# One page table instead of two, a first stage that turns while it mixes, and two engines' loops that begin in the middle of a group

## The chip, the cores and the metric

The kernel runs on one core of one Trainium2 chip. The metric is the device time of one execution in microseconds (us). A core has five engines with an instruction stream each: TensorE (PE in the rows; its weight loads are PEld), VectorE (DVE), ScalarE (ACT), GpSimd (POOL) and SyncE (SP), which here issues nearly all transfers. They meet by semaphores only.

## The reference

Four residual steps on `x` of 64 items x 32 rows x 512 columns:

```python
x = x + einsum('bct,bcd->bdt', x, W0[itok_B_0_15])            # L0: one 32x32 weight per item
x = x + x @ Wb.T + bias + (x @ A[id].T) @ B[id].T             # L1: base weight and a rank-16 adapter per item
x = x + attention(x, Wq, Wk, Wv, Wo, pages, table, seqlens)   # L2: 32 heads, 8 KV heads, D=128,
                                                              #     16 pages of 32 keys per item, RMS norm, rotation
x = x + einsum('bct,bcd->bdt', x, W3[itok_B_0_15])            # L3: one 32x32 weight per item
```

In L2 every item reads the 16 pages that its row of the block table names, masks the keys past its length, adds its own 32 keys, and takes a softmax over 544 keys for each of 32 heads.

## The kernel before, in words

The 64 items make 16 tiles of 4 items (4 x 32 = 128 rows). Each engine's whole program is written out by hand; what is long is a hardware loop (`Fori`) whose body is a stretch of straight code, with an unrolled piece ahead of it and behind it.

**First stage (L0 and L1).** 16 tiles, function `round1a` on each engine, four tiles to a pass; the loop runs over the passes. For tile t TensorE does `mix0` (one 128x512 matmul of x with the block-diagonal L0 weights `bd0`), VectorE `add0` adds x, giving x1; TensorE `turn1` transposes x1 in four pieces; ScalarE `x1_turned` and VectorE `x1_low` split the turned tile into two roundings; TensorE `base` multiplies with the adapter's A (four matmuls) and with the base weight (12 matmuls); `own_adapters` adds B; VectorE `add1` adds x1, giving x2; `turn2` transposes x2 for L2. TensorE takes the tiles in the order `mix0(t+2)`, `turn1(t+1)`, `base(t)`, `turn2(t-1)`, `own_adapters(t)`.

**Projections (L2).** Q, K and V of all tiles, stored to memory. Loops over two blocks of 512 output columns: ScalarE `block_qk` and VectorE `block_qk`.

**Attention (L2).** 16 groups of 4 items; an item has 8 units (one per KV head, with its 4 query heads), so a group has 32 units, u = 0 to 31 (`UG`). Every engine has a function `step(g, u)`. At step u TensorE computes the scores of unit u+2 (L1256), transposes the probabilities of unit u (L1137), does one or two matmuls of the previous group's output projection (L1320) and the values of unit u-1 (L1289; at an item's end L1273 and L1299 for its own keys). ScalarE takes the exponentials of unit u+1 and rounds the keys of unit u+4 (`split_k`, L730); VectorE makes the low part of the keys of unit u+3 (`split_k`, L1002), masks and takes the maximum of unit u+2 (L1017), and normalises unit u+1 (L1023, L1028, L1029). `split_q` makes the low and high parts of four units' queries (L1008, L738). `residual` (L1040) closes a group at u = 31. Group 0 and group 15 are straight code, groups 1 to 14 a loop; TensorE, ScalarE and VectorE all branch back after u = 31, GpSimd after u = 23.

**SyncE in attention.** Function `group(g, par, first, last)`, four items k = 0 to 3. For each it waits until the buffer of two items earlier is free, issues the query load (L388), the item's own keys (L384), reads 16 page numbers from a table in SBUF into registers (`load_pages`, L377), issues the 16 page loads (L379), its own values (L393), and the store of the outputs (L457). The 64 page numbers of a group stand in one of two tables `btab[:, par]`; the next group's table is loaded at k = 0. Because `par` alternates, the loop body holds two groups: 7 iterations for groups 1 to 14, so 6 branches back. Two buffers of pages alternate between items.

```python
group(0, 0, True, False)
with sp.Fori(0, NT // 2 - 1) as gg:
    group(gg * 2 + 1, 1, False, False)
    group(gg * 2 + 2, 0, False, False)
group(NT - 1, 1, False, True)
```

**Output stage.** The second half of the output projection, and L3.

Of the kernel before, what the change touches and what calls it, by code (L numbers as in the profile page):

```python
# [23 lines left out]
I32 = mybir.dt.int32  # L24
# [35 lines left out]
RESIDUAL = UG - 1  # L60
WO_SPLIT = 8
# [18 lines left out]
def build(nc, x, cond_row, id_row, bt_row, idx_pages, seq_tok, seq_all, w0, w3, wb, bias,  # L80
          lora_a, lora_b, wqk, wv, wo, qn, kn, kT_cache, v_cache, ident_c, iota_c, row_c, invf_c,
          hmask_c, out):
    ctx = ExitStack()
    with ctx:
# [51 lines left out]
        x1_sb = [inK(T) for _ in range(4)]  # L136
# [5 lines left out]
        w0_sb = inK(CONDS * C).rearrange("p (k d) -> p k d", k=CONDS)  # L142
        la_sb = inK(LORAS * HC * RANK).rearrange("p (k n) -> p k n", k=LORAS)
# [77 lines left out]
        btab = sb("btab", [1, 2, BT * NPP], I32)  # L221
# [34 lines left out]
        s_mm0, s_x1, s_tx1, s_x1T = sem("s_mm0"), sem("s_x1"), sem("s_tx1"), sem("s_x1T")  # L256
# [30 lines left out]
        s_w3 = sem("s_w3")  # L287
# [21 lines left out]
        def _(sp):  # L309
# [18 lines left out]
            for j in range(2):  # L328
                load_x(0, j)
            sp.dma_start(wb_sb, wb.rearrange("p c n -> p (c n)")).then_inc(s_wb, 16)  # L330
            sp.dma_start(la_sb, lora_a).then_inc(s_la, 16)
# [7 lines left out]
            for j in range(4):  # L339
                sp.wait_ge(s_x1, j + 1)  # L340
                load_x(1, j)
# [7 lines left out]
            with sp.Fori(2, NT // 4) as i:  # L349
                for j in range(4):  # L350
                    sp.wait_ge(s_x1, i * 4 - 3 + j)
                    load_x(i, j)
                    sp.wait_ge(s_mm1, i * 4 - 3 + j)
                    load_b(i, j)
            for dst, src in ((seqt[:], seq_tok), (invf, invf_c), (rowc[:], row_c), (qn_sb[:, 0, :], qn), (qn_sb[:, 1, :], kn),
                             (btab0[:], bt_row[:, 0:2 * NPP]), (btab[:, 0, :], bt_row[:, 2 * NPP:(2 + BT) * NPP]), (iota[:], iota_c), (seqi, seq_all), (idxi, idx_pages)):
# [81 lines left out]
            def group(g, par, first, last):  # L438
                for k in range(BT):
                    b = g * BT + (k + 2)  # L440
                    if not (last and k >= 2):
                        sp.wait_ge(s_qp, g * (2 * BT) + 2 * (k + 1))
# [8 lines left out]
                    if k == 1 and first:  # L451
                        sp.wait_ge(s_x2yst, 16)
                    elif k == 1:
                        sp.wait_ge(s_x2yst, g * 32 - 16 if last else g * 32)
# [18 lines left out]
            sp.wait_ge(s_x2yst, 32 * NT - 32)  # L473
# [24 lines left out]
            sp.wait_ge(s_x2yst, 32 * NT - 16)  # L498
# [110 lines left out]
        def _(act):  # L609
# [8 lines left out]
            def x1_turned(i, j):  # L618
                i, j, t = tile(i, j)
                act.wait_ge(s_tx1, t + 1)  # L620
                nc.scalar.copy(x1T_sb[j], bank[4]).then_inc(s_x1T, 1)
# [35 lines left out]
            for dst, src in ((ident[:], ident_c), (hmask, hmask_c)):  # L657
# [4 lines left out]
            act.wait_ge(s_w0, 16)  # L662
# [4 lines left out]
            act.wait_ge(s_wb, 16)  # L667
# [109 lines left out]
            def step(g, u):  # L777
# [15 lines left out]
                if u % 4 == 3 and not (fixed and n + 5 >= NU):  # L793
                    split_q(g * (UG // 4) + (u // 4 + 2), u + 5, g * 2 + (u + 5) // (2 * HK))
# [645 lines left out]
```

## Time and profile before

| what | value |
|---|---|
| median of 3 runs | 2315.6 us (2314.19 to 2317.2) |
| the profiled execution's own time | 2315.53 us |
| its span in the profile | 2313.8 us |
| TensorE busy | 2251.0 us, 97% of the span |
| VectorE busy | 1765.2 us, 76% |
| ScalarE busy | 1594.6 us, 69% |
| GpSimd busy | 557.0 us, 24% |

The span is the time between the first and the last recorded instruction; 1.7 us of the execution lie around it. A share of busy time is a mean over stages: it tells which engine to look at first, and the waits tell where it stands still.

### The profile page before, as it was taken

Reading aid. Unit: us, or ns where it says so; the run is one execution under the profiler, and the core shown is the slowest. Engines: PE = TensorE matmul, PEld = TensorE weight load, DVE = VectorE, ACT = ScalarE, POOL = GpSimd, SP = SyncE. Lnnn points to the kernel's source line nnn. Section 1 sums busy time; section 2 is a strip of 40 time slices with the busy share of each in tenths; the row PEclk is TensorE's granted clock in tenths of the full one; section 3 lists DMA queues with packets and bytes.
Section 4 is the critical chain, followed back from the end, with each engine's and each line's share of the span. In section 5 each row is a group of like instructions: output and inputs, shape, how many; then the busy total and the mean of one; then the engine's idle time right before and its main releaser. Section 6 shows DMA issues by size and latency. Waiting matters only on the chain.

```text
span 2313.8 us, 56498 instructions
## 1 busy us (share of the span) xinstructions
PE 2251.0 (97%) x15392; PEld 2008.7 (87%) x15392; DVE 1765.2 (76%) x5613; ACT 1594.6 (69%) x4413; POOL 557.0 (24%) x712
## 2 busy tenths in 40 slices
PE   8999999999999899999999999999999999999999
PEld 5778888888887899989989989989999989997777
DVE  3434777777777999889989989989989989995332
ACT  4423666666666988878878878878878878884221
POOL 1002444444443221221221222122122212210000
PEclk9999999999999999999999999999999999999999
DMA  5335333333327777777777777777777778765332
GB/s 169 95 97 172 105 102 101 100 101 103 116 82 236 245 260 265 258 238 259 257 235 257 256 243 249 259 254 248 254 252 257 250 238 263 245 227 182 135 122 97
DMA packets 347991, 456.02 MB, mean 197 GB/s; under 512 B 34538, under 2 KB 280874, under 8 KB 343726
## 3 DMA queue, kind: packets, MB, share of 16 engines
q1 hardware_dynamic: 308430, 315.83, 42.8%
q0 software_dynamic: 36864, 134.23, 16.6%
q10 hardware_dynamic: 2528, 4.29, 0.5%
q14 instruction: 135, 1.11, 0.2%
q8 instruction: 34, 0.56, 0.1%
HBM read 374.53 MB, written 79.69 MB: 196 GB/s over the span
## 4 chain that ended last, share of the span: by engine, by line
PE 80%; SPq 6%; issue 6%; DMA 3%; DVE 3%; ACT 2%; ACTq 0%; POOL 0%; DVEq 0%; POOLq 0%
PE oP L1289 14%; PE S L1256 13%; PE S L1213 11%; PE oP L1213 11%; PE S L1307 8%; PE bank L1137 8%; PE bank L1320 6%; SPq L379 3%; PE oP L1137 3%; PE oP L1167 2%; DMA regK<-kT_cache 2%; SPq L377 2%; PE oP L1299 1%; DVE k_lo L1002 1%; PE oP L1159 1%
## 5 line engine op out<-in xcount | busy, mean ns | idle before, releaser
L1289 PEld LDWEIGHTS oP<-regC,regK 128*128 128x128 f32 x4096 | 534.4, 193 | 36.9 <-issue 5.0
L1289 PE MATMUL oP<-regC,regK 128*128 128x128 f32 x4096 | 544.8, 276 | 1.3
L730 ACT CAST k_hi<-regK 128x544 fp32r<-128x544 f32 x512 | 331.5, 647 | 160.6 <-PE S L1256 127.4
L1017 DVE CUSTOM_DVE_ANT_0 regC<-S,mask 128x544 f32<-128x544 f32 x512 | 368.7, 720 | 66.5 <-issue 58.9
L1002 DVE TENSOR_TENSOR k_lo<-regK,k_hi 128x544 fp32r<-128x544 f32 x512 | 368.3, 719 | 35.3 <-ACT k_hi L730 35.0
L744 ACT ACTIVATE regC<-regC,nmx 128x544 f32<-128x544 f32 x512 | 387.9, 758 | 1.9 <-DVE nmx L1017 1.8
L1137 PE MATMUL bank<-ident,regC 128*128 128x128 f32 x2048 | 311.0, 275 | 24.5 <-ACT regC L790 24.5
L571 POOL TENSOR_TENSOR regC<-regC 128x256 f32<-128x256 f32 x320 | 245.6, 788 | 278.6 <-DVE regC L977 278.6
L790 ACT COPY regC<-bank 128x512 f32<-128x512 f32 x512 | 298.8, 584 | 5.5 <-PE bank L1137 5.5
L550 POOL COPY idx<-idx_all 128x4 int32 (+1 forms) x65 | 30.4, 470 | 1071.0 <-PE oP L1299 969.8
L553 POOL DMA_INDIRECT regK<-v_cache,idx x256 | 266.9, 1043 | 79.3 <-issue 79.1
L1137 PEld LDWEIGHTS bank<-ident,regC 128*128 128x128 f32 x2048 | 245.8, 142 | 25.8 <-issue 25.8
L1256 PE MATMUL S<-k_hi,q_hi 128*128 128x288 f32 (+1 forms) x1024 | 257.4, 332 | 9.4 <-DVE nmx L1017 8.7
L1029 DVE TENSOR_SCALAR regC<-regC,rinv 128x512 f32<-128x512 f32 x512 | 246.6, 482 | 0.0
L1256 PE MATMUL S<-k_hi,q_lo 128*128 128x288 f32 (+1 forms) x1024 | 214.4, 291 | 0.0
L1256 PE MATMUL S<-k_lo,q_hi 128*128 128x288 f32 (+1 forms) x1024 | 213.3, 290 | 0.0
L977 DVE SCALAR_TENSOR_TENSOR regC<-S,rstd,regK 128x128 f32<-128x128 f32 x640 | 172.8, 343 | 11.6 <-issue 2.9
L977 DVE SCALAR_TENSOR_TENSOR regC<-oP,rstd,regK 128x128 f32<-128x128 f32 x640 | 172.7, 342 | 8.3
L1256 PEld LDWEIGHTS S<-k_hi,q_hi 128*128 128x128 f32 x1024 | 155.8, 192 | 24.0 <-issue 10.3
L1213 PE MATMUL S<-w_hi,x2T_hi 128*128 128x512 f32 x384 | 157.9, 411 | 1.4 <-ACT regC L681 1.4
L1256 PEld LDWEIGHTS S<-k_hi,q_lo 128*128 128x128 f32 x1024 | 158.3, 190 | 0.0
L1256 PEld LDWEIGHTS S<-k_lo,q_hi 128*128 128x128 f32 x1024 | 157.9, 190 | 0.0
(136 smaller groups left out, 4319.5 us busy)
## 6 DMA issues: line engine op xcount, KB each, us to landing
regK<-kT_cache SPq DMA_DIRECT2D x1024, 128.0 KB
qkT_d<-regC SPq DMA_DIRECT2D x160, 256.0 KB, 2.3
regC<-qkT_d SPq DMA_DIRECT2D x64, 512.0 KB, 8.0
oT_d<-regC SPq DMA_DIRECT2D x64, 256.0 KB, 6.3
regK<-oT_d SPq DMA_DIRECT2D x16, 1024.0 KB, 5.4
regC<-wqk SPq DMA_DIRECT2D x10, 1024.0 KB, 5.3
v_d<-regC SPq DMA_DIRECT2D x32, 256.0 KB, 2.3
regK<-qkT_d SPq DMA_DIRECT2D x64, 128.0 KB
```

What stands on the lines that cost most here:

```text
L553: nc.gpsimd.indirect_dma_start(out=v_sb[par][:, m, :], out_offset=None, in_=v_cache, in_offset=bass.IndirectOffsetOnAxis(ap=idx[k][:, m:m ...
L730: nc.scalar.copy(k_hi[u % 2].rearrange("p (s t) -> p s t", t=PSIZE), k_sb[b][:, :, h, :]).then_inc(s_khi, 1)
L744: nc.scalar.activation(p, p, ACT.Exp, bias=nmx[:, u % 4:u % 4 + 1], scale=-1.0, accum_out=rs[:, u % 4:u % 4 + 1]).then_inc(s_exp, 1)
L790: nc.scalar.copy(pT_sb[u % 2], pT).then_inc(s_evA, 1)
L977: last = nc.vector.scalar_tensor_tensor(out=dst[t % 2][:, h, :], in0=bank[t % 4][:, h * D:(h + 1) * D], scalar=rstd[:, t % 4, h:h + 1], in ...
L1002: nc.vector.tensor_tensor(lo, k_sb[b][:, :, h, :], hi.bitcast(F32), ALU.subtract).then_inc(s_klo, 1)
L1017: nc.vector.tensor_tensor_reduce(out=p_sb[u % 4], in0=scores, in1=mask[:], scale=-SCALE, scalar=3e38, op0=ALU.add, op1=ALU.min, accum_out= ...
L1029: nc.vector.tensor_scalar(p[:, 0:L], p[:, 0:L], rinv[:, j:j + 1], None, ALU.mult).then_inc(s_p, 1)
L1137: last = nc.tensor.transpose(dst[:, c * P:(c + 1) * P], src[:, c * P:(c + 1) * P], ident[:])
L1213: last = nc.tensor.matmul(bank[t % 4], a[:, c, rows], w[k][:, cols], start=(c == 0 and m == 0), stop=(c == HC - 1 and m == 2))
L1256: last = nc.tensor.matmul(scores[:, at], q[u // 4 % 2][:, head], k[u % 2][:, at], start=(i == 0), stop=(i == 2))
L1289: last = nc.tensor.matmul(oP[:, at:at + P], v_sb[b][:, m, h * D:(h + 1) * D], pT_sb[u % 2][:, m * P:(m + 1) * P], start=(h < 4 and m == 0) ...
```

## The change

Five edits.

1. SyncE has one table `btab`. `load_table` moves from k = 0 to k = 3 (behind the last `load_pages` that reads the old table), counts on its own semaphore `s_tabin`, and SyncE waits for it at k = 0 of the next group. The body of the loop is one group: 14 iterations, 13 branches back.
2. First stage: the identity is added to the L0 weights (`eye`) and to the base weight (`ident`) once, so `add0` is gone and `add1` becomes a copy; `mix0` and `turn1` become `mixed`, four matmuls with x as the stationary side, which give x1 already turned. VectorE does `add1` ahead of `split_w` in the last pass. The base weight is loaded ahead of the second x tile.
3. ScalarE and VectorE: units 0 to 15 of group 1 are written out, and the loop body is units 16 to 31 of g and 0 to 15 of g+1 (`TURN`). TensorE's loop is as before.
4. ScalarE splits a group's last queries at u = 29 and no longer at 31.
5. VectorE does so at u = 30 and no longer at u = 0 of the next group.

```diff
+QUERIES_AT = (*range(3, UG - 1, 4), UG - 3)
+TURN = 16
...
-            def load_table(g, par, count):
-
-                sp.dma_start(btab[0:1, par, 0:count],
-                             bt_row[0:1, bass.ds(g * (BT * NPP) + 2 * NPP, count)]).then_inc(s_x2yst, 16)
+            def load_table(g):
+
+                sp.dma_start(btab[:], bt_row[0:1, bass.ds(g * (BT * NPP) + 2 * NPP, BT * NPP)]).then_inc(s_tabin, 16)
...
-            def group(g, par, first, last):
+            def group(g, first, last):
                 for k in range(BT):
                     b = g * BT + (k + 2)
                     if not (last and k >= 2):
+                        if k == 0:
+                            ge(sp, s_tabin, g * 16)
                         sp.wait_ge(s_qp, g * (2 * BT) + 2 * (k + 1))
                         load_q(b, k % 2)
                         sp.wait_ge(s_klo, g * UG + HK * (k + 1))
                         load_own_k(b, k % 2)
-                        load_pages(btab[0:1, par, k * NPP:(k + 1) * NPP], k % 2)
+                        load_pages(btab[0:1, k * NPP:(k + 1) * NPP], k % 2)
                         sp.wait_ge(s_po, g * BT + (k + 1))
                         load_own_v(b, k % 2)
-                    if k == 0 and not last:
-                        load_table(g + 1, 1 - par, BT * NPP)
+                    if k == 3 and not last:
+                        load_table(g + 1)
...
-            group(0, 0, True, False)
-            with sp.Fori(0, NT // 2 - 1) as gg:
-                group(gg * 2 + 1, 1, False, False)
-                group(gg * 2 + 2, 0, False, False)
-            group(NT - 1, 1, False, True)
+            group(0, True, False)
+            with sp.Fori(1, NT - 1) as g:
+                group(g, False, False)
+            group(NT - 1, False, True)
...
+            for u in range(TURN):
+                step(1, u)
             with dve.Fori(1, NT - 1) as g:
-                for u in range(UG):
+                for u in range(TURN, UG):
                     step(g, u)
-            for u in range(UG):
+                for u in range(TURN):
+                    step(g + 1, u)
+            for u in range(TURN, UG):
                 step(NT - 1, u)
...
-                if u % 4 == 0 and not (fixed and (n == 0 or n + 4 >= NU)):
+                if u % 4 == 0 and u > 0 and not (fixed and n + 4 >= NU):
                     split_q(g * (UG // 4) + (u // 4 + 1), u + 4)
+                if u == UG - 2 and not (fixed and n + 6 >= NU):
+                    split_q(g * (UG // 4) + (u // 4 + 2), u + 6)
...
-            def mix0(i, j):
+            def mixed(i, j):
+
                 i, j, t = tile(i, j)
                 pe.wait_ge(s_pick0[j], i * 4 + 4)
                 pe.wait_ge(s_xin[j], i * 16 + 16)
-                ge(pe, s_x1, t - 1)
-                nc.tensor.matmul(bank[j % 2], bd0[j], x_sb[j], start=True, stop=True).then_inc(s_mm0, 1)
-
-            def turn1(i, j):
-                i, j, t = tile(i, j)
-                pe.wait_ge(s_x1, t + 1)
-                ge(pe, s_x1T, t)
-                transposes(bank[4], x1_sb[j]).then_inc(s_tx1, 1)
+                ge(pe, s_x1T, t - 1)
+                for c in range(HC):
+                    at = slice(c * P, (c + 1) * P)
+                    last = nc.tensor.matmul(bank[4 * (j % 2)][:, at], x_sb[j][:, at], bd0[j], start=True, stop=True)
+                last.then_inc(s_tx1, 1)
```

SyncE's code around the branch back, between the last item of a group and the first of the next. Before, the end of the second group of the body (then it goes on at the first group's L388, L384, L377):

```order
L393 DMA regK<-v_d 32x256
L457 ISA
L457 DMA oT_d<-regC 128x512
L466 DMA x_d<-regC 128x512
L469 REGISTER_ALU
L469 COMPARE_AND_BRANCH
```

With the change, the end of the only group of the body:

```order
L394 DMA regK<-v_d 32x256
L374 ISA
L374 DMA btab<-bt_row 1x64
L458 ISA
L458 DMA oT_d<-regC 128x512
L467 DMA x_d<-regC 128x512
L470 REGISTER_ALU
L470 COMPARE_AND_BRANCH
```

The table's load now stands right ahead of the output store and the branch, and every group ends in the branch.

VectorE's code where the attention loop begins. Before, the body starts at unit 0, with a `split_q` in its first step:

```order
L1091 UNCONDITIONAL_BRANCH
L1091 ISA
L1002 TENSOR_TENSOR k_lo_69<-regK,k_hi_70 128x544
L1015 REGISTER_ALU
L1016 MEMSET hold 128x1
L1017 ISA regC,nmx<-S,mask 128x544
```

With the change it starts at unit 16, after 16 more units of straight code (the first rows of its body are the same five instructions of a step, with the change's line numbers):

```order
L1098 UNCONDITIONAL_BRANCH
L1098 ISA
L1005 TENSOR_TENSOR k_lo_69<-regK,k_hi_70 128x544
L1018 REGISTER_ALU
L1019 MEMSET hold 128x1
L1020 ISA regC,nmx<-S,mask 128x544
```

So the body lies at another place of VectorE's program, and its length is 309 instructions where it was 308. The built programs hold, between the start of a loop and its branch back: SyncE's attention loop 852 instructions before and 429 with the change; ScalarE's projection loop 399 and 399, its attention loop 260 and 261; VectorE's projection loop 402 and 402, its attention loop 308 and 309. An instruction is 64 bytes.

TensorE's code in a tile of the first stage. Before, one wide matmul (L1145) and four transposes (L1137, from `turn1`) ahead of the adapter's four (L1159):

```order
L1173 MATMUL oP<-regK 128x512
L1145 MATMUL S<-regK 128x512
L1149 REGISTER_ALU
L1137 MATMUL oP<-ident,regK 128x128 x4
L1159 MATMUL oP<-regK 64x128 x4
```

With the change, four matmuls of `mixed` in their place:

```order
L1180 MATMUL oP<-regK 128x512
L1157 MATMUL S<-regK 128x128 x4
L1162 REGISTER_ALU
L1166 MATMUL oP<-regK 64x128 x4
```

## Rows read from the trace of the kernel before

**Rows 1.** The page's chain of work that ended last, shares of the span by engine.

```profile
PE 80%; SPq 6%; issue 6%; DMA 3%; DVE 3%; ACT 2%; ACTq 0%; POOL 0%; DVEq 0%; POOLq 0%
```

**Rows 2.** The same chain in order of time: start us, us, what.

```profile
994.40 6.45 issue
1015.95 6.96 DMA regK<-kT_cache
...
1851.49 5.99 issue
```

**Rows 3.** Timeline of VectorE, the residual that closes groups 1, 2 and 14.

```profile
902.62 0.68 DVE L1040 TENSOR_TENSOR regC<-bank,regC 128x512 f32<-128x512 f32 x1
985.52 0.69 DVE L1040 TENSOR_TENSOR regC<-bank,regC 128x512 f32<-128x512 f32 x1
...
2015.88 0.69 DVE L1040 TENSOR_TENSOR regC<-bank,regC 128x512 f32<-128x512 f32 x1
```

**Rows 4.** Timeline of ScalarE at its projection loop's first branch back; brackets: idle before.

```profile
381.32 0.28 ACT L693 ACTIVATE regC<-oP 128x128 f32<-128x128 f32 x1 [4.30 <-issue]
```

**Rows 5.** Timeline of VectorE at its projection loop's branches back, both times.

```profile
372.29 0.18 DVE L972 RECIPROCAL rstd<-sd 128x4 f32<-128x4 f32 x1 [2.87 <-issue]
...
377.70 2.16 DVE L977 SCALAR_TENSOR_TENSOR regC<-S,rstd,regK 128x128 f32<-128x128 f32 x8 [2.89 <-issue]
...
474.62 0.18 DVE L972 RECIPROCAL rstd<-sd 128x4 f32<-128x4 f32 x1 [2.44 <-issue]
```

**Rows 6.** Timeline of VectorE where its attention loop branches back, after group 4.

```profile
1156.93 0.69 DVE L1040 TENSOR_TENSOR regC<-bank,regC 128x512 f32<-128x512 f32 x1
1157.53 0.72 DVE L1002 TENSOR_TENSOR k_lo<-regK,k_hi 128x544 fp32r<-128x544 f32 x1
```

**Rows 7.** The page's DMA queues: packets, MB, share of 16 engines.

```profile
q14 instruction: 135, 1.11, 0.2%
```

**Rows 8.** Timeline of SyncE, where the table's load is issued today.

```profile
1101.73 0.27 SPq L372 DMA_DIRECT2D btab<-bt_row  x1
1102.18 0.38 SPq L457 DMA_DIRECT2D oT_d<-regC  x1
```

**Rows 9.** Timeline of VectorE, group 4, steps 15 and 16.

```profile
1114.74 0.48 DVE L1029 TENSOR_SCALAR regC<-regC,rinv 128x512 f32<-128x512 f32 x1
...
1116.28 0.72 DVE L1017 CUSTOM_DVE_ANT_0 regC<-S,mask 128x544 f32<-128x544 f32 x1 [0.43 <-issue]
```

**Rows 10.** Timeline of TensorE in the same step, the transposes of unit 16.

```profile
1116.08 0.60 PE L1137 MATMUL bank<-ident,regC 128*128 128x128 f32 x4
```

**Rows 11.** Timeline of TensorE in one tile of the first stage.

```profile
23.71 1.02 PE L1145 MATMUL S<-regK 128*128 128x512 f32 x2
24.57 0.60 PE L1137 MATMUL oP<-ident,regK 128*128 128x128 f32 x4
25.10 1.09 PE L1159 MATMUL oP<-regK 128*64 128x128 f32 x8
26.12 0.50 PE L1167 MATMUL oP<-wb_hi,x1T_hi 128*128 128x512 f32 x1
...
30.28 1.02 PE L1145 MATMUL S<-regK 128*128 128x512 f32 x2
```

**Rows 12.** The chain in order of time, one step's values in attention.

```profile
961.67 0.89 PE oP L1289 x8
```

**Rows 13.** Timeline of VectorE, last tile of the first stage, ahead of `add1`.

```profile
120.56 1.28 DVE L897 TENSOR_TENSOR w_lo<-regC,w_hi 128x512 fp32r<-128x512 f32 x2
```

**Rows 14.** Timeline of TensorE from a group's last own-key transpose to the next scores.

```profile
1156.89 0.38 PE L1273 MATMUL bank<-ident,regC 128*128 128x128 f32 x2
1157.33 0.52 PE L1256 MATMUL S<-k_hi,q_hi 128*128 128x288 f32 x2
...
2015.84 0.38 PE L1273 MATMUL bank<-ident,regC 128*128 128x128 f32 x2
2016.00 0.49 PE L1256 MATMUL S<-k_hi,q_hi 128*128 128x288 f32 x2
```

More of the change, by code:

```diff
@@ L326, in load_b @@
                                  lora_b[bass.ds(rows[b], 1)].rearrange("a r n -> r (a n)")).then_inc(s_bin[j], 16)
-            for j in range(2):
-                load_x(0, j)
+            load_x(0, 0)
             sp.dma_start(wb_sb, wb.rearrange("p c n -> p (c n)")).then_inc(s_wb, 16)
+            load_x(0, 1)
             sp.dma_start(la_sb, lora_a).then_inc(s_la, 16)
@@ L445, in group @@
                         load_own_k(b, k % 2)
-                        load_pages(btab[0:1, par, k * NPP:(k + 1) * NPP], k % 2)
+                        load_pages(btab[0:1, k * NPP:(k + 1) * NPP], k % 2)
                         sp.wait_ge(s_po, g * BT + (k + 1))
                         load_own_v(b, k % 2)
-                    if k == 0 and not last:
-                        load_table(g + 1, 1 - par, BT * NPP)
[L451 to L454, printed above, removed]
+                    if k == 3 and not last:
+                        load_table(g + 1)
+                    if k == 1 and not first:
+                        ge(sp, s_x2yst, g * 16 - 16)
                         sp.dma_start(x2r, x2_d[bass.ds(g - 1, 1)].rearrange("a p n -> p (a n)")).then_inc(s_x2r, 16)
@@ L792, in step @@
                     split_k(n + 4, u + 4, g * 2 + (u + 4) // (2 * HK))
-                if u % 4 == 3 and not (fixed and n + 5 >= NU):
-                    split_q(g * (UG // 4) + (u // 4 + 2), u + 5, g * 2 + (u + 5) // (2 * HK))
+                if u in QUERIES_AT:
+                    v = (u // 4 + 2) * 4
+                    if not (fixed and g * UG + v >= NU):
+                        split_q(g * (UG // 4) + (u // 4 + 2), v, g * 2 + v // (2 * HK))
                 if u in HEADS_AT:
@@ L882, in add1 @@
                 ge(dve, s_x2st[j], i * 16)
[L883 removed]
+                nc.vector.tensor_copy(x2_sb[j], bank[2 + j % 2]).then_inc(s_x2, 1)
             def x2_low(i, j):
@@ L905, in round1a @@
                 for j in range(4):
-                    if not (last and j >= 2):
-                        add0(i, j + 2)
                     own_rank(i, j)
@@ L912, in round1a @@
                         x2_low(i, j - 1)
+                    add1(i, j)
                     if last:
@@ L915, in round1a @@
                             split_w(j // 2, j // 2, j % 2 * 2 + c)
-                    add1(i, j)
-            for j in range(2):
-                add0(0, j)
+            dve.wait_ge(s_const, 48)
+            dve.wait_ge(s_w0, 16)
+            nc.vector.tensor_tensor(w0_sb, w0_sb, eye.unsqueeze(1).to_broadcast([P, CONDS, C]), ALU.add).then_inc(s_w0i, 1)
+            dve.wait_ge(s_wb, 16)
+            for c in range(HC):
+                at = slice(c * T + c * P, c * T + (c + 1) * P)
+                nc.vector.tensor_tensor(wb_sb[:, at], wb_sb[:, at], ident[:], ALU.add).then_inc(s_wbi, 1)
             x1_low(0, 0)
@@ L1090, in _ @@
                     split_wo(0, u - WO_SPLIT, wo_lo, wo_raw)
+            for u in range(TURN):
+                step(1, u)
             with dve.Fori(1, NT - 1) as g:
-                for u in range(UG):
+                for u in range(TURN, UG):
                     step(g, u)
-            for u in range(UG):
+                for u in range(TURN):
+                    step(g + 1, u)
+            for u in range(TURN, UG):
                 step(NT - 1, u)
@@ L1143, in mix0 @@
                 pe.wait_ge(s_xin[j], i * 16 + 16)
[L1144 to L1151 removed]
+                ge(pe, s_x1T, t - 1)
+                for c in range(HC):
+                    at = slice(c * P, (c + 1) * P)
+                    last = nc.tensor.matmul(bank[4 * (j % 2)][:, at], x_sb[j][:, at], bd0[j], start=True, stop=True)
+                last.then_inc(s_tx1, 1)
             def base(i, j):
@@ L1184, in round1a @@
                 for j in range(4):
-                    if not (last and j >= 2):
-                        mix0(i, j + 2)
                     if not (last and j == 3):
-                        turn1(i, j + 1)
+                        mixed(i, j + 1)
                     if first and j == 0:
@@ L1197, in _ @@
             pe.wait_ge(s_ones, 4)
-            mix0(0, 0)
-            mix0(0, 1)
-            pe.wait_ge(s_const, 32)
-            turn1(0, 0)
+            mixed(0, 0)
+            pe.wait_ge(s_const, 48)
             round1a(0, True, False)
@@ L1427 @@
         "ident_c": np.eye(P, dtype=np.float32),
+        "eye_c": np.tile(np.eye(C, dtype=np.float32), (BT, 1)),
         "iota_c": np.tile(np.arange(L, dtype=np.float32), (P, 1)),
```

34 lines of the change are left out of this document (14 added, 20 removed).

## The prediction

> **What bounds the kernel now.** I read the page's chain first: TensorE holds 80% of it, "SPq" and "issue" together 12% [rows 1]. So TensorE is the bound nearly everywhere, and what is not TensorE lies in a few places. Put in order of time, the same chain shows where: six times in attention, from 994.40 to 1851.49, a piece called issue of 5.6 to 6.5 us, some 20 us later a piece that waits for a page load [rows 2]. These are the six branches back of SyncE's loop, after groups 2, 4, ... 12. Nothing that the profile shows ends such a piece, and the ordinary turn from item to item has none. SyncE then issues the next item's pages late; ScalarE cannot round its keys, and TensorE runs dry.
>
> The price is read from the ends of the groups. Group 2, with no branch of SyncE in it, takes 985.52 - 902.62 = 82.9 us. Groups 2 to 14 are 13 groups and take 2015.88 - 902.62 = 1113.3 us, against 13 x 82.9 = 1077.7 [rows 3]. The difference over six branches is 5.9 us each: the whole of SyncE's pause reaches TensorE. SyncE has no slack there, since its 16 register reads and 16 page issues fill most of the time for which a page buffer is free.
>
> What is the pause? At the branch back of ScalarE's projection loop (399 instructions) the engine stands 4.30 us [rows 4]; at those of VectorE's (402) 2.87 and 2.44 us [rows 5]. At the branch back of VectorE's attention loop (308) it does not stand at all: one instruction ends at 1157.62, the next has begun at 1157.53 [rows 6]. So bodies of 260 and 308 instructions go round free, and bodies of 399, 402 and 852 pay each time. That is what loading of code looks like, and there is a queue for it: 135 packets of 1.11 MB, which is 8.2 KB or 128 instructions each [rows 7]. I read the rows so: an engine holds some blocks of 128, has the next one loaded while it runs, and pays when a branch goes to a block that is gone. A body that touches three blocks stays; one that touches five is lost. Four is not in the trace.
>
> The Trainium skill ("Runtime: NRT & Kernel Launch", Instruction fetch mechanics) says that an engine other than TensorE holds 512 instructions in two blocks of 256, and that a taken branch out of that window waits for a load. By its figure SyncE's new body of 429 could fit, and the pauses would vanish; that is the rival below with the other sign. The trace agrees on the pause but not on the size: bodies of 399 and 402 did not stay.
>
> **The change, part by part.**
>
> *SyncE's loop.* The body shrinks from 852 to 429 instructions. That is more than the 399 and 402 that pay, so I expect it to pay as well, and now after each of groups 1 to 13: 13 branches in place of 6. Pause and stretch around it are the same (same waits, same free time of the buffer), so each costs 5.9 us: + 7 x 5.9 = + 41.3 us. Bounds of one: 5.0 and 7.2 us, the smallest and the largest pause 5.59 and 6.45 [rows 2] with half a microsecond to each side for what the next transfers add.
>
> *The table's load.* It stood at k = 0, where it costs 0.45 us of SyncE's issue time (1102.18 - 1101.73) [rows 8]. Now it stands ahead of the branch, in front of the late item: + 0.45 x 13 = + 5.9 us as long as SyncE pauses there. Behind it in the queue are the output store, the branch, and the next item's queries, keys and pages. The new wait for the table itself costs nothing: the pause of 6 us is longer than a small load. Without the pause it would cover 0 to 3 us, beside the wait for the key buffer that stands behind it. I take 0.
>
> *VectorE's loop begins at unit 16.* The new body has 309 instructions, as many as before, so the count says that it goes round free. The place says otherwise. In the projection loop a second pause of 2.89 us comes after a reciprocal, at the 15th or 16th instruction from the loop's start [rows 5]; I take that as the edge of a block. Counted on by 128 in the built program, the attention loop before began on an edge (within two instructions) and touched three blocks: free, as seen. The new loop begins about 10 instructions ahead of an edge and touches four. If four are too many, VectorE pauses at each of 13 branches. Price of one: 2.9 us in the projections [rows 5]; in attention the queues are fuller, and ScalarE's 4.3 there compares with SyncE's 5.9 here, so 2.9 + 1.6 = 4.5 us. TensorE has slack: the probabilities of unit 16 are ready at 1115.22 and used at 1116.08 [rows 9, 10], and VectorE idles 0.43 us in that step [rows 9], 1.3 us together. That leaves 3.2, and I add 0.8 for the second block, whose edge comes 10 instructions on and which cost 2.9 us in one of two cases [rows 5], partly hidden. 4.0 x 13 = + 52 us. Bounds: 2.44 - 1.3 = 1.1 (14 us), and 6.45 + 2.89 - 1.3 = 8.0 (104 us). ScalarE's new loop of 261 touches three blocks by the same count and stays free.
>
> *TensorE's gap at its own branch.* From the last own-key transpose to the next scores it takes 0.44 us at a branch back and 0.16 in group 15, where there is none [rows 14]. TensorE's loop still turns at unit 0, so the 0.28 stays: 0. If the other engines' branches had a part in it, - 0.28 x 13 = - 3.6.
>
> *Queries two units sooner.* One 128x512 operation each on ScalarE and VectorE moves by two units; both have some slack per unit and TensorE none. 0; at worst a delay of its 0.7 us less the 1.3 of slack, again 0.
>
> *First stage.* A tile takes 30.28 - 23.71 = 6.57 us and TensorE's starts follow without a gap. Out go L1145 (24.57 - 23.71 = 0.86) and the transposes (25.10 - 24.57 = 0.53) [rows 11]. In come four matmuls of 128 columns in full f32: the values of attention are four such and take 0.89 [rows 12], the adapter's four in this stage 1.02 (26.12 - 25.10) [rows 11]. I take 0.89, same columns and same weights' size. From the first `base` on, 13 `mix0`, 14 `turn1` against 14 `mixed`: - 11.2 - 7.4 + 12.5 = - 6.1 us (with 1.02: - 4.3). At the end `add1` no longer stands behind 1.28 us of weight splitting [rows 13]: - 1.2. At the start the identity has to be added before ScalarE can pick (a 128x512 operation, 0.68 us at the residual [rows 3], and a wait), but one `mix0` less precedes the first `base`: - 0.6 together, - 1.5 to + 1.5. Sum - 8 us, from - 10 to - 3.
>
> **Sum.** 2315.5 (the profiled execution's own time, 0.1 under the median of 2315.6) + 41.3 + 5.9 + 52 - 8 = 2406.7 us. I give 2407.
>
> **The rivals.**
>
> A. *SyncE pauses, VectorE does not* (one odd pause in the projections was something else, or a body of four blocks stays for an engine that runs only a third of the last). 2315.5 + 41.3 + 5.9 - 8 = 2355 us. For it: the edge rests on one pause of two.
>
> B. *SyncE's body stays loaded; no pauses.* Then the six of before are gone as well: 2315.5 - 6 x 5.9 - 8 = 2272 us, faster. It decides at whether an engine can keep four blocks and still go back to the first of them. For it: 429 is half of 852 and the only long body seen on SyncE was 852. Against it: 399 and 402 pay, on two engines. It also says that VectorE stays free.
>
> C. *SyncE free, VectorE not*: 2272 + 52 = 2324 us. It needs different limits on two engines.
>
> D. *The pauses double but fewer reach TensorE.* The 5.9 of before is the whole pause, six times out of six, so I give it no weight of its own; it lies in the lower part of A.
>
> **How the numbers follow.** Likeliest 0.56 (both pause), A 0.25, B 0.14, C 0.05. The likeliest alone runs from 2363 (VectorE 14 us, first stage - 3 to - 10) to 2460, mostly 2370 to 2440. To hold 8 in 10 the range takes in A (2335 to 2365) and leaves out B, C and the last of the upper tail: 2335 to 2450. A measurement of this kernel can tell about 0.2% (4.6 us) from no change. Faster by more than that is B, 0.14; within it nearly nothing, 0.02 (a part of C); slower 0.84.
>
> **What the profile of the changed kernel would show.** For SyncE: a piece called issue of 5.6 to 6.5 us after every group, and all 13 groups near 89 us or more, none at 82.9. Under B every group has 82.9 and the instruction queue fewer packets than 135; with doubled pauses it has about as many as before or more, since 13 x 4 blocks are loaded for 6 x 7. For VectorE: idle of 3 to 6 us ahead of the keys of unit 19, once in a group, and TensorE dry 3 us behind it; if the edge was misread, nothing there. For the first stage: a tile of 6.1 us. Wrong it would be above all if four blocks stay, or if the pause is not the loading of code but something of the two-group body.

## The result and the profile after

The changed kernel takes 2387.32 us (median of 4 runs, 2382.64 to 2391.02), the kernel before on the same chip 2314.89 us. The ratio is 1.0319, with a 95% interval of 1.0303 to 1.0335: 3.2% slower, some 72 us. I had given 2407 us, with a range from 2335 to 2450.

The page first: the chain that ended last, by engine, and the queue that loads instructions. They answer to [rows 1] and [rows 7].

```profile
q14 instruction: 203, 1.66, 0.2%
...
PE 57%; SPq 15%; issue 14%; DVE 6%; DMA 6%; ACT 2%; ACTq 0%; DVEq 0%
```

TensorE fell from 80% of the chain to 57%; what took its place is SyncE's queue and "issue", 29% together where 12% were. Instruction packets rose from 135 to 203. The chain in order of time (start us, us, what) shows where, and answers to [rows 2]:

```profile
820.25 5.85 DMA btab<-bt_row
842.35 7.50 DMA regK<-kT_cache
911.34 6.39 issue
933.68 8.03 DMA regK<-kT_cache
1004.18 5.71 issue
...
2008.11 5.70 issue
```

A piece called issue of 5.24 to 6.48 us now stands after each of 13 groups, and each is followed by a wait for a page load. The first two rows have no counterpart before: at 820.25, after group 0, SyncE waits for the page table itself.

The ends of groups 1, 2 and 14 on VectorE's timeline, which answer to [rows 3]:

```profile
903.22 0.68 DVE L1043 TENSOR_TENSOR regC<-bank,regC 128x512 f32<-128x512 f32 x1
996.35 0.68 DVE L1043 TENSOR_TENSOR regC<-bank,regC 128x512 f32<-128x512 f32 x1
...
2092.90 0.68 DVE L1043 TENSOR_TENSOR regC<-bank,regC 128x512 f32<-128x512 f32 x1
```

Groups 2 to 14 take 1189.7 us where they took 1113.3: + 76.4 us, more than the whole loss. A group lasts 91.5 us on average, and none 82.9.

One SyncE pause on its own timeline. The group's last store goes out at 910.50, the next item's queries only at 918.10:

```profile
910.02 0.38 SPq L458 DMA_DIRECT2D oT_d<-regC  x1
910.50 0.65 SPq L467 DMA_DIRECT2D x_d<-regC  x1
918.10 0.36 SPq L389 DMA_DIRECT2D regC<-qkT_d  x1
```

And VectorE's, after its branch back at unit 16. Its keys come 2.4 us late (in other groups up to 3.12), and TensorE, in the second fence, waits 0.72 and 0.24 us for the maximum:

```profile
1223.64 0.48 DVE L1032 TENSOR_SCALAR regC<-regC,rinv 128x512 f32<-128x512 f32 x1
1226.56 0.72 DVE L1005 TENSOR_TENSOR k_lo<-regK,k_hi 128x544 fp32r<-128x544 f32 x1 [2.44 <-ACT k_hi L730]
```

```profile
1228.08 0.49 PE L1259 MATMUL S<-k_hi,q_hi 128*128 128x288 f32 x2 [0.72 <-DVE nmx L1020]
...
1231.10 0.49 PE L1259 MATMUL S<-k_hi,q_hi 128*128 128x288 f32 x2 [0.24 <-DVE nmx L1020]
```

ScalarE is named as the releaser there, but it had written those keys 3.3 us earlier; with VectorE's loop moved by 40 instructions (vector_pad, below) the same keys follow ScalarE's by 0.75 us and VectorE does not stand.

A tile of the first stage, which answers to [rows 11]: 31.78 - 25.61 = 6.17 us, and `mixed` (L1157) holds TensorE for 26.59 - 25.61 = 0.98 us.

```profile
25.61 1.05 PE L1157 MATMUL S<-regK 128*128 128x128 f32 x8
26.59 1.09 PE L1166 MATMUL oP<-regK 128*64 128x128 f32 x8
...
31.78 1.05 PE L1157 MATMUL oP<-regK 128*128 128x128 f32 x8
```

The difference of the two spans, 2389.2 - 2313.8 = 75.4 us, split at VectorE's first maximum of unit 1 (726.5 against 733.5) and at the ends of groups: - 7.0 up to attention, + 7.6 in groups 0 and 1, + 76.4 in groups 2 to 14, - 1.6 behind, for which no run gives a cause.

### The profile page after: what moved, and what is told of

Read it like the earlier page. It is cut to its first block, busy times and chain, and to the rows that moved or that the text cites. A ratio compares the mean times of both kernels' runs of the same rounds, so it can differ in the third digit from the quotient of the medians.

```text
span 2389.2 us, 56602 instructions
## 1 busy us (share of the span) xinstructions
PE 2270.0 (95%) x15424; PEld 2032.8 (85%) x15424; DVE 1756.0 (73%) x5602; ACT 1602.0 (67%) x4413; POOL 557.3 (23%) x712
## 3 DMA queue, kind: packets, MB, share of 16 engines
q14 instruction: 203, 1.66, 0.2%
## 4 chain that ended last, share of the span: by engine, by line
PE 57%; SPq 15%; issue 14%; DVE 6%; DMA 6%; ACT 2%; ACTq 0%; DVEq 0%
PE S L1216 11%; PE oP L1216 11%; SPq L380 8%; PE S L1310 7%; PE oP L1292 7%; PE S L1259 6%; DMA regK<-kT_cache 4%; SPq L378 4%; PE bank L1146 4%; PE bank L1323 3%; PE oP L1146 3%; DVE k_lo L1005 2%; PE oP L1174 2%; DVE regC L1032 1%; SPq L394 1%
## 5 line engine op out<-in xcount | busy, mean ns | idle before, releaser
L1292 PEld LDWEIGHTS oP<-regC,regK 128*128 128x128 f32 x4096 | 541.3, 195 | 36.6 <-issue 3.8
L1292 PE MATMUL oP<-regC,regK 128*128 128x128 f32 x4096 | 551.6, 278 | 0.1
L1146 PE MATMUL bank<-ident,regC 128*128 128x128 f32 x2048 | 317.6, 279 | 65.8 <-ACT regC L790 65.8
```

What stands on the lines that cost most here:

```text
L1146: last = nc.tensor.transpose(dst[:, c * P:(c + 1) * P], src[:, c * P:(c + 1) * P], ident[:])
L1292: last = nc.tensor.matmul(oP[:, at:at + P], v_sb[b][:, m, h * D:(h + 1) * D], pT_sb[u % 2][:, m * P:(m + 1) * P], start=(h < 4 and m == 0) ...
```

## The experiments

All in one table first. Each median is of 3 to 12 runs; the ratio is to the kernel before on the same chip, with its 95% interval. "Groups" is the mean length of groups 2 to 14 in the profiled run, from the ends as above; "idle" is how much of it TensorE stands idle, and the rest it is busy; "packets" is the instruction queue's count on the page.

| kernel | median us | ratio | groups us | of it idle us | packets |
|---|---|---|---|---|---|
| before | 2315.6 | 1 | 85.6 | 2.0 | 135 |
| after | 2387.3 | 1.0319 (1.0303 to 1.0335) | 91.5 | 5.9 | 203 |
| sync_pair | 2334.8 | 1.0091 (1.0072 to 1.0111) | 88.0 | 3.8 | 195 |
| turn_zero | 2347.0 | 1.0148 (1.0121 to 1.0175) | 88.3 | 3.5 | 203 |
| vector_pad | 2355.7 | 1.0185 (1.0161 to 1.0208) | 89.1 | 4.4 | 137 |
| first_only | 2309.3 | 0.9981 (0.9972 to 0.9991) | 85.7 | 1.9 | 131 |
| table_halves | 2361.5 | 1.0208 (1.0194 to 1.0223) | 89.6 | 4.8 | 151 |
| sync_straight | 2269.6 | 0.9807 (0.9794 to 0.9821) | 82.7 | 0.0 | 108 |
| sync_items | 2268.6 | 0.9804 (0.9790 to 0.9818) | 82.7 | 0.0 | 68 |
| before_pad | 2319.7 | 1.0026 (1.0014 to 1.0038) | 86.3 | 3.0 | 201 |
| vector_alone | 2299.1 | 0.9942 (0.9928 to 0.9955) | 85.0 | 1.9 | 133 |
| vector_turn_zero | 2326.7 | 1.0069 (1.0045 to 1.0094) | 86.5 | 2.8 | 133 |
| head_order | 2266.7 | 0.9794 (0.9780 to 0.9807) | 82.8 | 0.0 | 68 |

The idle times are from windows over groups 2 to 14. Here in this order before, after, sync_items, vector_pad, vector_alone, turn_zero and vector_turn_zero: the window, its length, what TensorE was busy of it (then the other engines), and third from the end the granted clock:

```profile
902.62:2015.88 1113.26, 1087.48 (x9051) 1040.21 (x9050) 985.00 (x3187) 919.37 (x2029) 235.94 (x260) 0.99 0.76 252
903.22:2092.90 1189.68, 1112.37 (x9052) 1060.11 (x9051) 982.77 (x3187) 925.66 (x2029) 236.03 (x260) 0.97 0.72 236
894.90:1970.63 1075.73, 1075.43 (x9050) 1030.41 (x9051) 982.54 (x3186) 919.47 (x2028) 230.72 (x260) 1.00 0.80 260
900.83:2059.23 1158.40, 1101.00 (x9050) 1052.24 (x9051) 983.99 (x3186) 919.12 (x2028) 231.10 (x260) 0.98 0.74 242
896.10:2001.69 1105.59, 1080.62 (x9052) 1032.27 (x9051) 980.76 (x3187) 925.69 (x2029) 234.17 (x260) 1.00 0.78 253
901.12:2048.89 1147.77, 1102.79 (x9051) 1056.79 (x9052) 985.09 (x3187) 925.01 (x2029) 235.26 (x260) 0.97 0.76 244
895.68:2020.59 1124.91, 1089.07 (x9051) 1043.29 (x9052) 983.62 (x3187) 924.46 (x2029) 234.08 (x260) 0.98 0.76 249
```

The matmuls are the same in all of them, and without a pause they take 82.7 us a group. What a kernel is busy beyond that is matmuls that run slower.

### One part undone or done alone

**sync_pair: SyncE's two-group loop and two tables back.**

```diff
-            with sp.Fori(1, NT - 1) as g:
-                group(g, False, False)
+            with sp.Fori(0, NT // 2 - 1) as gg:
+                group(gg * 2 + 1, 1, False, False)
+                group(gg * 2 + 2, 0, False, False)
```

> The changed kernel with one thing undone: SyncE's attention loop has two groups in a body again (853 instructions) and two page tables, each loaded a group ahead. Theory (every branch back of SyncE costs 5.9 us or more of TensorE's time, and the table of group 1 is waited for in the open after group 0): 7 branches fewer (7 x 7 = 49 us), about 6 us back at group 1, so 2387 - 55 = 2332 us; what is left over the kernel before is VectorE's pause less the first stage's gain. Rival (VectorE's loop at unit 16 is the larger part, 52 us, as I predicted, and SyncE's the smaller): 2315 + 52 - 8 = 2359 us.

It came to 2334.8 us, near the 2332 expected. The groups alternate again, 84.5 to 85.5 us without a branch of SyncE and 90.4 to 91.9 with one. SyncE's part is the larger one, and the two-group loop had been the better of the two. What stays over the kernel before, some 2 us, is in every group, so it isn't SyncE's. Groups 0 and 1 take 895.4 - 725.9 = 169.5 us, as before (169.1) and not 176.7 as in the changed kernel: the loss there went with the single table.

**turn_zero: VectorE's and ScalarE's loops turned at unit 0.**

```diff
-TURN = 16
+TURN = 0
```

> The changed kernel with the loops of VectorE and ScalarE turned at unit 0 again (TURN = 0), all else kept. VectorE's body is then instructions 1495 to 1805 of its program; the kernel before had it at 1502 to 1811. Theory (what counts is where the body lies among the blocks of 128, whose edges I place at 1502 to 1504): it begins 8 ahead of an edge, still touches four blocks, and pauses, now ahead of the first units: 2375 to 2390 us. Rival (turning at unit 16 is itself what costs, because of what VectorE does there): the pause is gone, 2387 - 21 = 2366 us or less.

At 2347.0 us it lay below both figures; by time alone it would fall to the rival ("2366 us or less"). The trace says otherwise. The packets are still 203, VectorE still stands 2.2 to 2.7 us once a group, now ahead of the keys of unit 3, so its loop still loads its code each round, and it is not the unit that makes it do so. What fell is the price of SyncE's pause. SyncE's program is unchanged and it still pauses after each of the 13 groups, 5.9 to 7.1 us between the last store and the next queries:

```profile
1173.41 0.37 SPq L467 DMA_DIRECT2D x_d<-regC  x1
1180.33 0.36 SPq L389 DMA_DIRECT2D regC<-qkT_d  x1
```

But in all groups but one its late item is no longer waited for (steps 14 and 15 last 2.8 and 2.65 us, where they last 7.2 and 4.9 in the changed kernel). A group loses 5.5 us at its start instead. TensorE there, and a stretch of it by the view of windows (us, busy us of each engine, PEclk):

```profile
1169.86 0.49 PE L1259 MATMUL S<-k_hi,q_hi 128*128 128x288 f32 x2 [1.66 <-DVE nmx L1020]
...
1171.88 1.11 PE L1146 MATMUL bank<-ident,regC 128*128 128x128 f32 x4 [1.03 <-DVE regC L1032]
```

```profile
1171.90:1177.50 5.60, 5.60 (x26) 5.60 (x27) 4.00 (x15) 3.06 (x7) 2.46 (x2) 0.50 0.95 310
```

Two waits of 1.66 and 1.03 us, and then 5.6 us in which the granted clock is 0.50, 1.2 of 2.4 GHz: the four transposes take 1.11 us and not 0.60.

**first_only: the kernel before with the new first stage.** (24 one-element memsets on VectorE keep its attention loop within three blocks.)

> The kernel before with the new first stage alone (and 24 one-element memsets on VectorE in group 0, so that its attention loop stays within three blocks as before, at 1518 to 1827). What I predicted: - 8 us, 2307 us. What the changed kernel's trace shows: the projections begin 4.3 us sooner, so 2311 us; SyncE's six pauses stay.

2309.3 us, between the two figures, a ratio of 0.9981 (0.9972 to 0.9991): 2 to 6 us faster. In its profile attention begins 7.2 us sooner than before, 5.0 of it from the start of the projections (118.2 against 123.3) and the rest within them.

### Is it the blocks of code?

**vector_pad: the changed kernel with VectorE's loop moved by 40 instructions.**

```diff
                 step(0, u)
...
+                if u >= 12:
+                    for i in range((u - 12) * 2, (u - 12 + 1) * 2):
+                        nc.vector.memset(pad[:, i % 8:i % 8 + 1], 0.0)
```

> The changed kernel with 40 one-element memsets on VectorE in group 0, ahead of the loop, two a unit. The loop stays at unit 16 and keeps its 309 instructions, but now lies at 1659 to 1969, in three blocks by my count of the edges. Theory (place among the blocks): VectorE's idle of 2.9 us ahead of the keys of unit 19 is gone in all groups, TensorE loses nothing there, 2387 - 21 = 2366 us. Rival (the turn at unit 16, or the count of 309 against 308): no change, 2387 us.

The kernel got 40 instructions longer and 31.6 us faster, 10 more than expected. The page's queue:

```profile
q14 instruction: 137, 1.12, 0.2%
```

66 packets fewer than 203, which is 13 rounds of 5 and one. Apart from SyncE's late item, none of VectorE's keys in these groups wait longer than 0.20 us. So the pause is the loading of code, and the place of the loop decides it, with the body and its turning unit unchanged.

**before_pad: the same cause put into the kernel before.** 100 memsets, so that its loop straddles four blocks.

> The kernel before with 100 one-element memsets on VectorE in group 0, so that its attention loop, unchanged in length and turned at unit 0, lies at 1602 to 1911, in four blocks by my count. Theory (place among the blocks, and pauses of two engines at the same place of a group overlap, as in turn_zero, where VectorE's pause at unit 0 cost 5.6 us a group and SyncE's then nothing): the 7 groups that SyncE enters without a branch get 5.6 us longer, the 6 others stay near 88.5: 2313 + 7 x 5.6 = 2352 us. If the pauses add: 2313 + 13 x 5.6 = 2386 us. Rival (the length or the unit matters, not the place): 2313 us.

```profile
q14 instruction: 201, 1.65, 0.2%
```

66 packets more than 135: the place does it, in this kernel too. The price was wrong by a factor of four: a group without a branch of SyncE takes 84.1 to 84.6 us, 1.4 more than 82.9, and the whole kernel is 2319.7 us, where 2352 was expected. TensorE waits 1.08 and 0.31 us, and its clock stays at 1.00:

```profile
1166.23 0.49 PE L1260 MATMUL S<-k_hi,q_hi 128*128 128x288 f32 x2 [1.08 <-DVE nmx L1018]
...
1168.86 0.49 PE L1260 MATMUL S<-k_hi,q_hi 128*128 128x288 f32 x2 [0.31 <-DVE nmx L1018]
```

```profile
1166.00:1172.00 6.00, 5.47 (x45) 5.34 (x46) 5.89 (x21) 5.11 (x13) 4.61 (x4) 1.00 0.84 230
```

**How large is a block?** The built programs give six places of VectorE's loop, all 309 or 310 instructions long with the branch. Begun at instruction 1502 (before), 1518 (first_only) or 1659 (vector_pad) it goes round free; begun at 1495 (turn_zero), 1602 (before_pad) or 1619 (the changed kernel) it loads five packets a round. Blocks of 128 of which three stay fit all six, with an edge between 1496 and 1502. The obvious rival, blocks of 256 of which two stay, fits vector_pad and before_pad as well, but not all: the body begun at 1495 touches three such blocks only with an edge in 1496 to 1549, the one begun at 1602 only with an edge in 1603 to 1655, and edges 256 apart can't be in both.

**table_halves: vector_pad with the table loaded in two halves, each two items ahead of its use.**

```diff
-                    if k == 3 and not last:
-                        load_table(g + 1)
+                    if k % 2 == 1 and not last:
+                        load_table(g + 1, k // 2, s_x2yst if k == 3 else s_tabin)
```

> The kernel vector_pad (VectorE's loop within three blocks) with the page table loaded in two halves: the entries of a group's items 0 and 1 go out for the next group right after item 1's pages, two items ahead of their use; those of items 2 and 3 after item 3's. Theory (what group 1 lost in the changed kernel, 5.9 us against the kernel before, is the wait for a table that was asked for one item too late; after the later groups SyncE's pause covers it): group 1 back to 82.5 us, the other groups as in vector_pad (88.9 us) or up to 0.5 us shorter, 2355.7 - 5.9 = 2350 us. Rival (group 1 lost to something else, such as the straight code of VectorE and ScalarE up to unit 16): 2356 us.

Group 1 gave back 4.5 of the 5.9 us expected: its end moved from 900.8 to 896.3 us, and sync_pair's is at 895.4. In the changed kernel SyncE issues the table's load at 820.25 and the queries that wait for it at 826.37:

```profile
820.25 0.55 SPq L374 DMA_DIRECT2D btab<-bt_row  x1
820.85 0.85 SPq L458 DMA_DIRECT2D oT_d<-regC  x1
826.37 0.36 SPq L389 DMA_DIRECT2D regC<-qkT_d  x1
```

The kernel as a whole did not get faster than vector_pad but 6 us slower in the median (the intervals of the ratios just overlap), 11 over the expectation; in the profile each of the other groups took 0.5 us more. What of that is the second load's issue and what the longer body, these runs do not tell.

It settles one thing more. The open wait for the table (5.85 us) and SyncE's pause (5.24 to 6.48) are about as long, so in the changed kernel the one could have passed for the other. Here the table of items 0 and 1 goes out two items ahead, and SyncE pauses all the same, 6.6 to 8.2 us between the last store and the next queries.

**sync_straight: table_halves with SyncE's groups written out.**

```diff
-            with sp.Fori(1, NT - 1) as g:
+            for g in range(1, NT - 1):
                 group(g, False, False)
```

> The kernel table_halves with SyncE's attention groups written out, no branch back (6,327 instructions in its program in place of 1,764). Theory (a pause is what a branch to code that is no longer held costs; straight code is loaded ahead, as between the loops): all 13 groups at 82.9 us, 2350 - 13 x 6.0 = 2272 us. Rival (SyncE's late item comes from the work at a group's end itself, the table, the two x2 transfers and the output store, not from the branch): 2350 us.

2269.6 us, 2.4 below the expectation, and every group from 2 on takes 82.7 or 82.8 us. The same work at each group's end costs nothing without the branch. With it a group takes 89.57 - 82.73 = 6.8 us more; no other pair of runs differs in the branch alone. Four and a half thousand more instructions are loaded in passing for 108 packets in all.

**sync_items: vector_pad with a loop of SyncE over two items.** The page numbers are loaded per item, one pair ahead; ScalarE issues the residual's two transfers of a group.

```diff
+            with sp.Fori(1, B // 2 - 1) as i:
+                two_items(i, False)
...
+                if u == 3 and not (fixed and g < 2):
+                    act.wait_ge(s_x2y, g - 1)
+                    act.dma_start(x2_d[bass.ds(g - 2, 1)].rearrange("a p n -> p (a n)"), x2r).then_inc(s_x2yst, 16)
```

> The kernel vector_pad with SyncE's attention loop over two items instead of a group's four: a body of 219 instructions at 888 to 1107, in two blocks by my count, 30 branches back; each item's table entries are loaded one item pair ahead, and the residual's two transfers a group go to ScalarE's queue. Theory (blocks of code): none of the 30 branches pauses, groups at 82.9 us, 2272 us (up to 2278 if ScalarE's two DMA issues a group delay a unit). Rival (a branch back of SyncE costs some 6 us whatever the body's length): 30 pauses, 2313 + 24 x 6 = 2457 us.

30 branches back, none of which shows: 2268.6 us, 2.0% under the kernel before. The page, and one group of it by windows beside the changed kernel's groups 2 and 3:

```profile
q14 instruction: 68, 0.56, 0.1%
...
PE 94%; DVE 2%; issue 2%; DMA 1%; ACT 1%; ACTq 0%; SPq 0%; DVEq 0%
```

```profile
895.00:978.00 83.00, 82.99 (x699) 79.52 (x700) 75.81 (x246) 70.97 (x158) 17.71 (x20) 1.00 0.81 260
```

```profile
903.22:996.35 93.13, 86.14 (x698) 82.08 (x697) 75.56 (x246) 71.23 (x157) 18.31 (x20) 0.96 0.71 232
996.35:1087.24 90.89, 84.84 (x699) 80.81 (x698) 75.57 (x246) 71.13 (x157) 18.22 (x20) 0.98 0.73 238
```

TensorE is busy for all of the 83 us. In the changed kernel's group 2 it is idle 93.13 - 86.14 = 7.0 us and, with the same matmuls, busy 3.2 us longer, at a mean clock of 0.96. About a third of what the two pauses cost in this group is not waiting but a slower clock behind the wait.

### The price of VectorE's pause

**vector_alone: sync_items without the memsets.** SyncE never pauses, VectorE does at unit 16.

> The kernel sync_items without the 40 memsets: SyncE never pauses, VectorE's loop lies as in the changed kernel (unit 16, four blocks). It prices VectorE's pause by itself, the term that I had put at 4.0 us a branch. From the groups of sync_pair that had no pause of SyncE (84.5 to 85.5 us against 82.75) I expect 2.3 us a branch: 2268.6 + 13 x 2.3 = 2298.5 us. Rival (the prediction's price, a longer pause where SyncE's doesn't cover part of it): 2268.6 + 52 = 2321 us.

2299.1 us, 0.6 from the expectation. VectorE's idle is 2.7 to 3.1 us once a group. The groups take 85.04 us, 2.3 more than in sync_items: TensorE stands idle for 1.9 of them and is busy 0.4 longer, all at a granted clock of 1.00. Taken by steps (means over groups 2 to 13): those of units 17 to 19 last 2.2 us more together, that of unit 31 0.36 more, that of unit 2 0.27 less.

**vector_turn_zero: the same with VectorE's loop turned at unit 0**, begun 8 instructions ahead of an edge. ScalarE's stays at unit 16, other than in turn_zero.

> The kernel vector_alone with VectorE's loop turned at unit 0 (309 to 310 instructions, begun 8 ahead of a block's edge), ScalarE's left at unit 16; SyncE never pauses. In turn_zero a group lost 5.6 us at its start, about half of it in matmuls at the lower granted clock behind the wait, and SyncE's late item was then not seen. Theory (that loss is VectorE's alone, and it covered SyncE's pause, which falls at the same place): groups of 88.2 to 88.4 us again, 2268.6 + 13 x 5.5 = 2340 us, close to turn_zero. Rival (SyncE's pause had a part in it, and VectorE's alone costs the 1.4 us of before_pad): 2268.6 + 18 = 2287 us.

2326.7 us (2318.5 to 2343.7), the profiled one being the fastest: neither. VectorE's pause alone costs more here than at unit 16 or in before_pad, but 1.8 us a group less than all together in turn_zero. Its groups in the profile run from 84.7 to 88.4 us, and the two kinds differ in the clock. The short kind and the long kind, two rows of windows in which the clock is the third number from the end:

```profile
1248.50:1252.00 3.50, 3.50 (x31) 3.50 (x32) 3.43 (x14) 2.89 (x7) 2.09 (x3) 1.00 0.94 326
1852.80:1856.50 3.70, 3.70 (x17) 3.70 (x18) 2.63 (x8) 1.87 (x4) 1.28 (x2) 0.50 0.96 316
```

TensorE had waited 1.22 and 0.78 us ahead of the first, 1.68 and 1.47 us ahead of the second.

### The head of the program

**head_order: sync_items with two of ScalarE's four first picks behind the rounding of the base weight.**

> The kernel sync_items with ScalarE's order at the very start changed: two of the four picks, then the first tile's two copies and the rounding of the base weight, then the other two picks. The first base matmuls wait for the weight's low part, which waits for ScalarE. Theory (the picks stand in that path, 2 x 1.7 us, and so the head gained nothing from the one matmul less in front of it): base starts 3.0 to 3.4 us sooner, 2268.6 - 3 = 2265.5 us. Rival (the head is bound by the load of the weight or gives the gain back through picks that now come late): 2268.6 us within 1 us.

```profile
16.41 1.94 PE L1175 MATMUL oP<-regK 128*64 128x128 f32 x8 [3.71 <-POOL regK L533]
```

The first `base` starts at 16.41 and no longer at 17.93: 1.5 us, half of what was expected, because GpSimd's picks end last then. The median, 2266.7, is 1.9 below that of sync_items, but they were measured on different chips and their intervals (0.9780 to 0.9807 and 0.9790 to 0.9818) overlap: no gain is shown.

## Why the prediction was right, and where not

**SyncE's pauses: right in number and in price, the price partly by luck.** A body of 429 instructions did not stay, so rival B fell; what the Trainium skill ("Runtime: NRT & Kernel Launch", Instruction fetch mechanics) gives as held for such an engine is not what the traces show here. The six places of VectorE's loop, above, rule it out wherever its blocks begin. The 13 pauses are 5.24 to 6.48 us. With the 0.45 for the table's issue I had 6.35 us a branch; vector_pad against sync_items, which differ in SyncE's loop and the residual's transfers, gives 89.11 - 82.75 = 6.36, table_halves against sync_straight 6.8. No run tests the 0.45 alone. (The bounds of one that I gave, 5.0 and 7.2, are 5.1 and 6.95 by their own working.)

My reading of the price was wrong: "the whole of SyncE's pause reaches TensorE", "SyncE has no slack there". Groups 2 and 3 of the kernel before, without and with a branch of SyncE:

```profile
902.62:985.52 82.90, 82.79 (x699) 79.28 (x698) 75.72 (x246) 70.71 (x157) 18.12 (x20) 1.00 0.80 260
985.52:1074.10 88.58, 84.23 (x699) 80.45 (x698) 75.79 (x247) 70.70 (x157) 18.16 (x20) 0.98 0.74 243
```

In group 3 TensorE stands idle 88.58 - 84.23 = 4.35 us and is busy 1.4 longer with the same matmuls, at a mean clock of 0.98. Over the six branches it is 4.1 us of waiting and 1.9 of slower matmuls each. So nearly 2 us of a pause of 6 never reach TensorE, and the slower clock behind the wait puts about as much on top. The two cancel, and the sum looked like the pause itself. The changed kernel repeats it (4.4 and 2.0 in vector_pad), which is why the price carried over.

**"The new wait for the table itself costs nothing": wrong at one place.** It holds where the loop branches back, 13 times. Group 0 is straight code, nothing pauses after it, and the load issued 0.6 us ahead of the next item is waited for in the open: 5.85 us of SyncE, 7.6 us at the end of group 1, where TensorE's clock also falls behind the wait (granted 0.50 from 850.1 to 856.9). I had bounded the wait without a pause by 0 to 3 us, and had not asked where there is no pause.

**VectorE's loop: the mechanism right, the size off.** Four blocks are one too many, and the place sets it; vector_pad and before_pad show this from both sides. The term was 4.0 us x 13 = 52. It measures 91.51 - 89.11 = 2.4 us beside SyncE's pauses and 2.3 alone, 31 us. Three steps of its working failed. "In attention the queues are fuller", + 1.6: the idle of VectorE is 2.4 to 3.1 us, as in the projections. And the second block, + 0.8, shows only as 0.36 us in the step of unit 31. The slack of 1.3 us was too large: steps 17 to 19 get 2.2 us longer by an idle of 2.9, so 0.7 was free. I had forecast TensorE dry for 3 us behind the pause; it waits 1.9 us a group in vector_alone.

**TensorE's own branch and the queries: 0 and 0, right together.** Groups without any pause take 82.75 us in sync_items and took 82.9 before; no run tests the two apart.

**First stage: - 8, within its bounds, but about half of it.** By the trace the projections begin at 118.94 and no longer at 123.26 us, - 4.3, and that is all that the term priced. Another 2.7 is gained in the projections and the first units behind them, where I had nothing; no run gives its cause. By the ratio of first_only the whole is - 4.4 (- 6.5 to - 2.1). `mixed` takes 0.98 us and not 0.89 (I had 1.02 as the other bound), so a tile 6.17 and not 6.10. At the head there was nothing to win by one matmul less: TensorE waits there for others (for VectorE's low part of the weight, and behind head_order's edit for GpSimd).

**The sum.** 2315.5 + 45.2 (SyncE, 13 x 6.36 = 82.7 less the 37.5 that six branches had cost) + 31.2 (VectorE, 13 x 2.4) + 7.6 - 7.0 - 1.6 = 2390.9, and the profiled execution took 2391.0. That it closes proves little, since the terms are differences of the same profiles; what tests them is that vector_alone, sync_straight and sync_items came within 4 us of figures given for them beforehand. The forecast of 2407 was 16 over the sum: 21 too much for VectorE, 2 too much for SyncE, 7.6 missing for the table, the rest in the ends. Two errors of opposite sign brought it nearer than its terms were. Without the wait for the table the kernel would stand near 2380, about as close to rival A's 2355 as to 2407; that VectorE pauses is shown by its idle and the packets, not by the time.

What stays open: why turn_zero costs 20 us more than vector_turn_zero. In the one both engines pause at a group's start, in the other VectorE alone; ScalarE's loop and SyncE's program differ too. Of the 1.8 us a group, 0.7 is TensorE waiting longer and 1.1 matmuls at the lower clock. Whether the two loads of code hinder each other, or what else makes the waits longer, no run here tells.

## What to carry to other kernels

Ask of every hardware loop how many instructions its body has and where it begins. Here a body within three blocks of 128 goes round free and one that touches a fourth pays 1.9 to 6.5 us on its engine at each branch back. Look for pieces of "issue" that recur with the loop and at the packets of the instruction queue, and try a shorter body, straight code or a shift of a few instructions. Halving a body that is still too long doubles the pauses.

A price read as "the engine's pause equals the group's loss" can be two things that cancel. Split the loss into waiting and slower work before you carry it over.

A wait that is hidden behind a stall is free only while the stall is there. Ask at each round of the loop, the first above all, whether it is.

## What I had not expected of the hardware

Forty added instructions made a kernel 31.6 us faster (vector_pad). A loop of VectorE's that doesn't stay costs five packets of code a round, four for the blocks that it touches and one more.

Pauses of two engines at the same place of a group do not add. In turn_zero both pause, and the groups take 88.3 us; with SyncE's alone they take 89.1, with VectorE's alone 86.5.

The price of a short wait of TensorE depends on what the clock does behind it. After waits of 1.08 and 0.31 us (before_pad) the granted clock stayed at 1.00, after 1.66 and 1.03 (turn_zero) it stood at 0.50 for over 5 us, and these groups lost 1.4 and 5.5 us: as much as the waits in the one case, twice as much in the other.
